# Where the seventh image's attention outputs are computed: in the next image's norm, and half a tile at each energy

## The reference, cut to what matters

```
x = x + softmax_rows(q k^T * dh^-0.5) v  w_proj + b_proj     # layer 0: 8 heads, windows of 32 tokens
q = gn(x) Wq; k = gn(x) Wk; v = gn(x) Wv                     # layer 1: one head, d = 32, all 1024 tokens
x = x + gamma * softmax(k q^T) v
```

## Time and profile before

| what | value |
|---|---|
| median of 3 runs | 689.38 us (687.95 to 689.65) |
| the profiled execution's own time | 689.47 us |
| its span, first to last instruction | 687.7 us |
| TensorE busy | 593.7 us (86%), 5859 matmuls |
| VectorE busy | 473.2 us (69%) |
| ScalarE busy | 349.5 us (51%) |
| GpSimd busy | 196.9 us (29%) |
| mean granted TensorE clock | 0.945 |

### The profile page before, as it was taken

The page is one execution under the profiler, slowest core; times in us unless marked ns, Lnnn a source line. Parts: engine busy times, 40 slices in busy tenths (PEclk is TensorE's granted clock), DMA queues, the critical chain, the costliest instruction groups (busy, mean ns, idle before and its releaser), DMA issues.

```text
span 687.7 us, 15145 instructions
## 1 busy us (share of the span) xinstructions
PE 593.7 (86%) x5859; PEld 429.9 (63%) x5859; DVE 473.2 (69%) x765; ACT 349.5 (51%) x486; POOL 196.9 (29%) x194
## 2 busy tenths in 40 slices
PE   2475587689999999999999999999999999649987
PEld 2254265346877677757775777668776767327756
DVE  4445246868886878687868788688868794664562
ACT  2522425097518852686348652875278513651363
POOL 5602221132046023513342314420460342001203
PEclk9795798599999999999999999999999999879999
DMA  5042132212332332243042323224223132201101
GB/s 160 0 124 62 43 83 82 62 38 64 108 74 66 78 93 71 63 108 93 23 107 76 84 61 92 68 57 112 68 68 82 33 74 64 72 1 39 49 0 62
DMA packets 40308, 47.53 MB, mean 69 GB/s; under 512 B 6848, under 2 KB 32320, under 8 KB 40256
## 3 DMA queue, kind: packets, MB, share of 16 engines
q1 hardware_dynamic: 36960, 43.47, 24.0%
q10 hardware_dynamic: 3296, 3.34, 1.4%
HBM read 10.09 MB, written 8.39 MB: 27 GB/s over the span
## 4 chain that ended last, share of the span: by engine, by line
PE 64%; DVE 16%; ACT 6%; issue 5%; SPq 4%; DMA 3%; POOL 1%; ACTq 0%; DVEq 0%; POOLq 0%
PE pb L253 9%; PE pb L254 8%; PE pb L255 8%; PE pa L253 7%; PE pa L255 6%; PE pa L254 6%; PE pa L491 4%; DVE max_neg L925 4%; PE pb L557 4%; PE pa L464 3%; PE pb L539 3%; SPq L321 3%; DVE ast L827 2%; PE pa L393 2%; PE pb L393 2%
## 5 line engine op out<-in xcount | busy, mean ns | idle before, releaser
L253 PE MATMUL pb<-v_h,e_h 128*128 128x257 f16 x464 | 127.5, 275 | 0.0
L255 PE MATMUL pb<-v_h,e_l 128*128 128x257 f16 x464 | 126.5, 273 | 0.0
L254 PE MATMUL pb<-v_l,e_h 128*128 128x257 f16 x464 | 126.1, 272 | 0.0
L925 DVE TENSOR_REDUCE max_neg<-pb 128x1 f32<-128x1024 f32 x64 | 77.5, 1211 | 55.6 <-PE pb L539 55.1
L940 DVE TENSOR_TENSOR e_l<-e,e_h 128x1024 f16<-128x1024 f32 x64 | 77.8, 1223 | 17.1 <-ACT e L749 15.5
L758 ACT ACTIVATE qk_h<-pb,y_fac 128x256 f32<-128x256 f32 x58 | 27.5, 474 | 109.9 <-DVE y_fac L947 109.6
L1097 POOL TENSOR_TENSOR y<-qk_h,y 128x256 f32<-128x256 f32 x64 | 46.3, 727 | 118.1 <-ACT qk_h L758 118.0
L749 ACT ACTIVATE e<-pb,f_energy 128x1024 f32<-128x1024 f32 x64 | 71.3, 1114 | 16.1 <-PE pb L557 16.1
L1078 POOL TENSOR_TENSOR xb<-xin,bias 128x2048 f32<-128x2048 f32 x8 | 36.7, 4588 | 125.9 <-DVE x L905 125.9
L1083 POOL TENSOR_TENSOR before_turn<-before_turn,a_rinv 128x1024 f32<-128x1024 f32 x16 | 30.6, 1912 | 128.3 <-DVE a_rinv L886 128.3
L253 PE MATMUL pa<-a_nh,wqkv_h 128*128 128x512 f16 x128 | 49.9, 389 | 13.1 <-DVE before_turn L896 7.3
(11 more groups left out here) (136 smaller groups left out, 1373.4 us busy)
## 6 DMA issues: line engine op xcount, KB each, us to landing
xin<-in_x SPq DMA_DIRECT2D x16, 512.0 KB, 4.6
diag<-qkT SPq DMA_DIRECT2D x64, 128.0 KB, 2.3
diag<-turned SPq DMA_DIRECT2D x64, 128.0 KB, 2.4
turned<-before_turn SPq DMA_DIRECT2D x128, 64.0 KB, 2.0
out<-y SPq DMA_DIRECT2D x24, 256.0 KB, 2.1
out<-y ACTq DMA_DIRECT2D x8, 256.0 KB, 2.1
q_stack<-qk_hl SPq DMA_DIRECT2D x8, 128.0 KB, 2.3
k_stack<-qk_hl SPq DMA_DIRECT2D x8, 128.0 KB, 2.4
```

What stands on the lines that cost most here:

```text
L253: nc.tensor.matmul(out_ap, lh, rh, start=start, stop=False)
L254: nc.tensor.matmul(out_ap, lh, rl, start=False, stop=False)
L255: return nc.tensor.matmul(out_ap, ll, rh, start=False, stop=stop)
L925: nc.vector.tensor_reduce(max_neg[:, it:it + 1], pb[:, 0:2, :].rearrange("p a n -> p (a n)"), X, ALU.max, negate=True).then_inc(b_max, 1)
```

## The change

The seventh image (b = 6) is treated apart, too. Its tiles 0 to 3 get the four banks of pa and are computed in `second(6)`: tiles 0 and 1 jt by jt behind the column energies 3 to 6 (jt 0 to 3), then jt 4 to 6 ahead of the group mean, jt 7 ahead of the group variance, with jt 0 and 1 of tiles 2 and 3; the rest of tiles 2 and 3 after the group variance. In `first(7)` only tiles 4 to 7 are left, in banks 2 and 3 of pb, and half a tile (12 matmuls) stands at each energy; the wait for the scale of tile it - 2 stays for tiles 6 and 7. For the last image tiles 6 and 7 go to banks 0 and 1 of pb, and wait for the last exponential in place of the scale of tiles 0 and 1. Only TensorE's list and `result_bank` change; the lists of the other engines stay as they are.

```
@@ -257,11 +257,15 @@
         def last_image(b):
             return isinstance(b, int) and b == IMAGES - 1
 
+        def next_to_last(b):
+            return isinstance(b, int) and b == IMAGES - 2
+
         def result_bank(b, it):
 
             if last_image(b):
-                it = it % 6
-                return pa[:, it, :] if it < 4 else pb[:, it - 2, :]
+                return pa[:, it, :] if it < 4 else pb[:, (it - 2) % 4, :]
+            if next_to_last(b) and it < 4:
+                return pa[:, it, :]
             return pb[:, 2 + it % 2, :]
 
         def out_banks(g):
@@ -564,7 +568,12 @@
                     pe.wait_ge(b_el, nth(b, 8, jts[-1] + 1))
 
                     if it >= 6:
-                        pe.wait_ge(b_part, nth(b, 8, it - 5))
+                        pe.wait_ge(b_exp, nth(b, 8, 8))
+                elif next_to_last(b) and it < 4:
+                    pe.wait_ge(b_el, nth(b, 8, jts[-1] + 1))
+                elif next_to_last(b):
+                    if it >= 6:
+                        pe.wait_ge(b_part, nth(b, 8, it - 1))
                 elif jts[0] == 0:
                     pe.wait_ge(b_el, nth(b, 8, 8))
 
@@ -582,9 +591,10 @@
             def first(i, b, o, m, f):
 
                 for it in range(4):
-                    if o and not last_image(i - 1): b_output(i - 1, it, b, range(0, 4))
+                    if o and b and not next_to_last(i - 1): b_output(i - 1, it, b, range(0, 4))
+                    if next_to_last(i - 1): b_output(i - 1, 4 + it // 2, b, range(it % 2 * 4, it % 2 * 4 + 4))
                     if b and it == 2: b_energy(i, 1, m)
-                    if o and not last_image(i - 1): b_output(i - 1, it, b, range(4, 8))
+                    if o and b and not next_to_last(i - 1): b_output(i - 1, it, b, range(4, 8))
                     if f and it == 1: transposes("a", i + 2, range(4))
                     if b and it >= 1: b_energy(i, (0, 2, 3)[it - 1], m)
                 for it in range(4, 8):
@@ -592,22 +602,24 @@
 
                         if it >= 6: b_output(i - 1, it, b)
                         continue
-                    if o: b_output(i - 1, it, b, range(0, 4))
+                    if next_to_last(i - 1): b_output(i - 1, 4 + it // 2, b, range(it % 2 * 4, it % 2 * 4 + 4))
+                    elif o: b_output(i - 1, it, b, range(0, 4))
                     if m and it == 5: a_output(i + 1, f, 0)
                     if f and it == 5: group_var("a", i + 2)
                     if m and it == 6: a_output(i + 1, f, 1)
                     if b and it == 7: b_energy(i, it, m)
-                    if o: b_output(i - 1, it, b, range(4, 8))
+                    if o and not next_to_last(i - 1): b_output(i - 1, it, b, range(4, 8))
                     if b and it < 7: b_energy(i, it, m)
                     if f and it == 4: group_mean("a", i + 2)
 
-            def outputs_behind(b, jts):
+            def outputs_behind(b, jts, its=range(6)):
 
                 for jt in jts:
                     if jt == 0:
 
                         pe.wait_ge(b_vl, nth(b, 4, 4))
-                    for it in range(6):
+                        pe.wait_ge(a_ol, nth(IMAGES, 2, 0))
+                    for it in its:
                         b_output(b, it, False, (jt,))
 
             def second(i, b, o, m, f):
@@ -625,15 +637,19 @@
                 if b: b_energy_T(i, 3)
                 if f: a_project_qk(i + 2, 1, (0,))
                 if last_image(i): outputs_behind(i, (0,))
+                if next_to_last(i): outputs_behind(i, (0,), (0, 1))
                 if b: b_energy_T(i, 4)
                 if b and f: b_project_v(i, (3,))
                 if last_image(i): outputs_behind(i, (1,))
+                if next_to_last(i): outputs_behind(i, (1,), (0, 1))
                 if f: a_project_qk(i + 2, 1, (1,))
                 if b: b_energy_T(i, 5)
                 if last_image(i): outputs_behind(i, (2,))
+                if next_to_last(i): outputs_behind(i, (2,), (0, 1))
                 if m: a_projection(i + 1, f, (0, 1))
                 if b: b_energy_T(i, 6)
                 if last_image(i): outputs_behind(i, (3,))
+                if next_to_last(i): outputs_behind(i, (3,), (0, 1))
                 if m: a_projection(i + 1, f, (2,))
                 if m: transposes("b", i + 1, (0, 1))
                 if m: a_projection(i + 1, f, (3,))
@@ -643,9 +659,14 @@
                 if f: a_project_qk(i + 2, 1, (3,))
                 if m: transposes("b", i + 1, (2, 3))
                 for j in range(4):
+                    if next_to_last(i) and j == 0: outputs_behind(i, (4, 5, 6), (0, 1))
                     if m and j == 2: group_var("b", i + 1)
                     if f: a_project_v(i + 2, (j,))
                     if m and j == 0: group_mean("b", i + 1)
+                    if next_to_last(i) and j == 0:
+                        outputs_behind(i, (7,), (0, 1))
+                        outputs_behind(i, (0, 1), (2, 3))
+                    if next_to_last(i) and j == 2: outputs_behind(i, range(2, 8), (2, 3))
                 if f: a_scores(i + 2)
                 for c in range(CHUNKS):
                     if m: b_project_qk(i + 1, f, c)
```

## The result

The changed kernel takes 693.31 us (median of 4, 691.25 to 694.03) against 688.66 us of the kernel before (4 runs, 687.82 to 689.65): ratio 1.006, 95% interval 1.0042 to 1.0077. Timed again in a second series it is 693.5 against 689.63 us, ratio 1.0052 (1.0033 to 1.0072). The profiled execution took 691.25 us, the fastest of all but one; its span is 689.4 us.

What follows compares the result with a forecast made beforehand. TensorE was taken as the bound among the eighth image's energies, waiting for the norm before them. Projection +1.3, energies +0.15, their clock +2.0, hand-over -0.45: +3.0 us on 689.4, 692.4 us; range 688.7 to 695.5.

Steps and rivals of the forecast that it cites:

- The energies: Eighth image's energies: energies 4 and 6 late behind scales of tiles 4 and 5; 18.5 us against 18.35, +0.15 us.
- The rival in which the energies step at 2.01 us: Tile 4's factor ahead of maximum 3, so no stalls: 14.07 instead of 18.5 us, 684.3 us in all; chance 0.08.
- Their clock: Clock falling in idle times before energy 0, tile 6 and tile 7: bounds 0 and 4.8 us, taken as +2.0.
- The variance: Norm: 18 matmuls ahead of the group variance delay it from 611.16 to 612.2 (+1.0 us), or 614.0 at 1.2 GHz.
- Part 1: Outputs of tiles 0 and 1 behind column energies keep the clock high; group mean 1.5 us earlier, 0 if it falls.
- Projection to energy 0: Variance to projection copy 6.4 + 1.5 us, then 5.42 us of copy, VectorE and DMA, unchanged, to the first energy.
- Hand-over: Energy 7 to first column energy: rows at +3.5 instead of +3.9 us, so the column energy 0.45 us earlier.
- tail: Last image: tiles 6 and 7 change banks and wait for exponentials already done; 0 us.
- the fall of 1.7 us under the 18 matmuls: Norm: low clock under matmuls ahead of the variance, 16 x 0.105 = 1.7 us, turning the projection's -0.45 into +1.3.

Runs made afterwards that it cites:

- c1_filler: Changed kernel plus matmuls nobody reads in idle times before energy 0 and tiles 6 and 7; 690.22 us, kernel before 689.63.
- c3_order2: Changed kernel with VectorE's factors 3 and 4 ahead of maximum 3 and factor 5 ahead of maximum 5; 685.69 us, kernel before 690.02.
- both mends: Changed kernel with tiles 6 and 7 in banks 0 and 1 of pa, and 18 matmuls moved behind the group variance; 682.94 and 682.13 us in two series.
- after: First profile of the changed kernel, nothing altered; that execution took 691.25 us.
- c1_after: Changed kernel again, unaltered, in a second series; 693.5 us, kernel before 689.63, ratio 1.0033 to 1.0072.
- c2_late: Changed kernel with 18 matmuls moved behind the group variance and 18 outputs moved into the idle time before energy 0; 689.37 us, kernel before 689.63.
- c2_warm: Kernel before plus 6 matmuls nobody reads behind each of the seventh image's column energies 3, 4 and 5; 689.35 us against 689.63.
- c3_warm2: Kernel before plus unread matmuls in the seventh image: 18 behind column energy 2, 6 each behind 3, 4 and 5; 687.02 us against 690.02.
- c1_order: Changed kernel with VectorE's factors 0 to 4 ahead of maximum 0, factors 5 to 7 also reordered; 689.19 us, kernel before 689.63.
- c3_best: Both mends plus 18 matmuls nobody reads behind column energy 2 of the seventh and eighth images; 682.67 us, kernel before 690.02.
- c3_both: Repeat of the changed kernel with both mends; 682.13 us, kernel before 690.02, ratio 0.9856 to 0.9916.
- c1_banks: Changed kernel with the seventh image's tiles 6 and 7 in banks 0 and 1 of pa; 685.82 us, kernel before 689.63.

## Why the prediction was right

The forecast was +3.0 us and 692.4; measured were +4.65 and 693.31 (+3.9 in the second series), inside the range of 688.7 to 695.5. Both stages that were to lose lost, by the waits that the prediction names. Point by point:

- **The energies (+0.15 without the clock).** Right to 0.1 us: energy 4 at 4.39 and energy 6 at 4.02 us where the clock holds (c1_filler), against 4.45 and 4.05. The rival in which the energies step at 2.01 us did not come true here, but it was right as to its condition and nearly as to its price: with the factor of tile 4 ahead of maximum 3 (c3_order2) the stage takes 14.43 us and the kernel 685.69, against 14.07 and 684.3; with both mends the stage takes 14.02.
- **Their clock (+2.0).** Too small: 2.8 and 2.9 us in the two profiles of the changed kernel, 1.34 and 1.40 at energy 0, 1.2 at tile 6 and 0.3 behind it. The prediction took one of the two falls in full and a part of the other; both came. The wait for tile 7 dropped the clock in none of the three profiles that have it as it is (after, c1_after, c2_late).
- **The variance (+1.0, or +2.8 at the low clock).** Right in both forms: from the mean (607.4) to the variance (612.2 or 614.0) it had 4.8 us at the high and 6.6 at the low clock; measured are 4.68 and 6.34. Which one comes is a matter of the execution: the forecast counts the low one, the profile of 691.25 us has the high one.
- **Part 1 (-1.5).** Right in one of the two profiles and mis-sized in the other. It said "With 6 matmuls more in each idle time I take it to stay high". In c1_after it did, and the gain was the 1.51 us of the forecast; in the profile of 691.25 us the clock fell at 590.88, and the gain was 0.74 us. Over the changed kernel and its variants it held in two of nine profiles, and c2_warm, the 6 matmuls alone, is 0.3 us faster, within the noise; c3_warm2 shows what was missing.
- **Projection to energy 0.** Variance to energy 0 was worked out as 13.3 us (7.9 to the copy, 5.4 after it), and is 13.41 to 13.43 in seven of the profiles of the changed kernel and its variants (14.07 in c1_order; 14.49 and 14.59 in c1_filler and c3_best, where the clock is low under the 36 outputs).
- **Hand-over (-0.45) and tail (0).** -0.40 and -0.13.

The profile c1_after is the case that the forecast counts, clock high under the column energies and low under the 18 matmuls. It adds up to +3.64 instead of +3.0: the stage of the energies is 0.85 us over its terms, by its clock, and the others together are 0.2 under theirs. In the profile of 691.25 us the near hit (+2.66) is luck: part 1 was 0.8 us too hopeful and the energies' clock 0.8 too small, and the fall of 1.7 us under the 18 matmuls, which was counted and did not come, made up for them. The execution of c1_after took 694.54 us, 5.1 us more than the profiled one of the kernel before, and 1.4 of them lie ahead of column energy 2 of the seventh image, where the two kernels do the same; no term of the forecast stands for that, and what makes it stays open.

## What to carry to other kernels

Work moved off an engine that is the bound gives only what the next chain leaves: here the stage could fall to seven maxima, 14.0 us, but in-order queues had put a scale behind a maximum, and with the outputs thinned out the scale was late. Before thinning work out, follow each wait that "was long done" and ask who releases it in the new order; then another bank costs nothing, and neither does an earlier place in the list, as long as it sets off no transfer beside one that is waited for. And ahead of a small matmul that a norm hangs on, put nothing: 18 matmuls there cost 2.5 to 4.4 us from the mean to the variance.

## What the runs showed of the hardware

- The clock's price depends on the execution. The same c1_order took from 683.75 us (mean granted clock 0.966) to 693.12 us (0.943) in 12 runs, and c1_filler 687.67 (0.970) to 693.26 (0.948); c3_both, whose idle time before energy 0 is 0.8 us and in which no energy waits behind a scale, 681.11 to 683.5 in 6. Which gaps drop the clock differed between two profiles of one kernel (at 590.88, under the column energies, in one; at 611.5, under the 18 matmuls, in the other).
- After the same idle time of 2.38 us, a column energy and 6 matmuls the clock fell in c2_warm and in the profile after, and held in c1_after and c1_banks. The 2.09 us before tile 7 dropped it in none of three profiles.
- With two stores of 256 KB issued behind 64 KB moves between partitions, the last move landed after 2.7 instead of 2.0 us (c1_order, c1_banks).
- Column energy 2 of the seventh image, up to which all these kernels are alike, came between 586.46 and 590.33 us. What makes that difference was not tried.
